# Gapped number row, convolution bias added once, and gather transfers written out one by one

## The reference, cut to what matters

```python
x = x + _L0_gnn_ref(h, ...)   # per edge a two-layer softplus MLP on h[dst] and edge_attr_64, summed by dst
x = x + _L1_gnn_ref(h, ...)   # message = A[type] @ h[src], summed by dst, then a GRU cell on the node
x = x + _L2_gnn_ref(h, ...)   # interaction of p1[src], p1[dst] with 8 basis values, tanh, summed by dst
x = x + _L3_gnn_ref(h, ...)   # two SAGE convolutions

def _sage_conv(x, edge_index, W_l, b, W_r):
    agg = segment_sum(x[src], dst); cnt = segment_sum(ones, dst)
    return (agg / clip(cnt, 1)) @ W_l + b + x @ W_r
h = relu(_sage_conv(x, edge_index, W1_l, b1, W1_r))
return _sage_conv(h, edge_index, W2_l, b2, W2_r)
```

## Time and profile before

| | us |
|---|---|
| median of 3 runs | 7642.43 |
| range of these runs | 7638.81 to 7652.46 |
| the profiled execution | 7640.1 |
| its span, first to last instruction | 7638.6 |
| busy: PE | 6650.0 (87%) |
| busy: POOL | 5038.0 (66%) |
| busy: DVE | 4913.9 (64%) |
| busy: ACT | 3097.5 (41%) |

### The profile page before, as it was taken

One profiled execution on the slowest core, in us unless ns is written; L12 is line 12 of the kernel. 1 busy time (PEld: TensorE's weight loads), 2 busy tenths in 40 slices (PEclk: granted clock), 3 DMA queues, 4 the chain that ended last, 5 costly groups with the idle time before them and its releaser, 6 DMA issues.

```text
span 7638.6 us, 166704 instructions
## 1 busy us (share of the span) xinstructions
PE 6650.0 (87%) x35133; PEld 3361.7 (44%) x35133; DVE 4913.9 (64%) x16097; ACT 3097.5 (41%) x5005; POOL 5038.0 (66%) x6109
## 2 busy tenths in 40 slices
PE   6999999956777777777769999999999899998998
PEld 4666666533333333333323444444444344443443
DVE  7777777646777777777746777777777733332332
ACT  4777777634445555455523333333333201110000
POOL 4544545257777777777747777777777376654776
PEclk9999999975665655665679999999999999998999
DMA  4333333332222222222222222222222266665765
GB/s 125 107 106 107 106 106 107 114 108 85 83 83 84 86 82 87 83 82 85 85 48 59 62 61 61 62 60 61 60 60 62 69 177 172 167 168 157 200 195 156
DMA packets 773997, 769.60 MB, mean 101 GB/s; under 512 B 242490, under 2 KB 585591, under 8 KB 773815
## 3 DMA queue, kind: packets, MB, share of 16 engines
q1 hardware_dynamic: 575703, 589.32, 24.8%
q0 software_dynamic: 147776, 160.99, 10.6%
q10 hardware_dynamic: 50400, 17.87, 1.0%
HBM read 581.15 MB, written 187.29 MB: 101 GB/s over the span
## 4 chain that ended last, share of the span: by engine, by line
PE 58%; POOL 12%; issue 12%; DVE 9%; DMA 4%; DVEq 2%; ACT 2%; ACTq 0%; POOLq 0%; SPq 0%
POOL zone L1045 9%; PE ps L2394 7%; PE ps L2555 7%; PE ps L2184 7%; PE ps L2202 6%; PE ps L2209 5%; PE ps L2386 4%; PE ps L2560 4%; DMA zone<-tab_msg,idx 3%; POOL zone L1085 3%; PE ps L2358 2%; DVE zone L1378 2%; PE ps L2200 2%; PE ps L2413 2%; PE ps L2404 1%
## 5 line engine op out<-in xcount | busy, mean ns | idle before, releaser
L1045 POOL DMA_INDIRECT zone<-tab_msg,idx x1664 | 1721.4, 1034 | 526.9 <-issue 462.3
L1045 POOL DMA_INDIRECT zone<-tab_u,idx x1664 | 1580.7, 950 | 600.1 <-issue 479.9
L2024 ACT ACTIVATE zone<-ps 128x792 fp8e4<-128x792 f32 x1200 | 963.3, 829 | 981.6 <-PE ps L2358 967.8
L1378 DVE TENSOR_TENSOR zone<-ps,zone 128x512 f32<-128x512 f32 x1664 | 1064.0, 686 | 367.0 <-PE ps L2386 335.6
L2184 PE MATMUL ps<-zone 128*128 128x64 f32 (+1 forms) x6656 | 839.2, 284 | 330.1 <-DMA zone<-tab_msg,idx 325.6
L2358 PE MATMUL ps<-zone 128*128 128x396 bf16 x2400 | 905.5, 488 | 234.2 <-ACT zone L2024 146.1
L2184 PEld LDWEIGHTS ps<-zone 128*128 128x128 f32 (+1 forms) x6656 | 758.2, 198 | 490.4 <-issue 438.2
L2394 PE MATMUL ps<-zone,w_bas 128*64 128x512 f32 x3328 | 899.1, 619 | 0.0
L2555 PE MATMUL ps<-zone 128*128 128x512 fp8e4 x3332 | 844.3, 383 | 24.4 <-DMA zone<-adj 14.0
L1663 DVE TENSOR_SCALAR zone<-tT,zone 128x392 bf16<-128x392 f16 x2400 | 779.3, 325 | 0.0
L1337 DVE SCALAR_TENSOR_TENSOR zone<-zone,ps 128x512 f32<-128x512 f32 x832 | 567.0, 687 | 269.8 <-ACT zone L1925 166.9
(11 more groups left out here) (323 smaller groups left out, 8824.5 us busy)
## 6 DMA issues: line engine op xcount, KB each, us to landing
zone<-adj SPq DMA_DIRECT2D x238, 768.0 KB
adj<-zone SPq DMA_DIRECT2D x150, 784.0 KB
zone<-in_dst_row SPq DMA_DIRECT2D x832, 128.0 KB, 2.7
zone<-in_ea_T SPq DMA_DIRECT2D x416, 128.0 KB, 2.6
zone<-src_lin SPq DMA_DIRECT2D x2448, 0.5 KB
zone<-adj SPq DMA_DIRECT2D x34, 896.0 KB
tab_msg<-zone SPq DMA_DIRECT2D x104, 256.0 KB, 2.1
zone<-tab_msg,idx POOLq DMA_INDIRECT x1664
```

The source lines that it names most:

```text
L1045: nc.gpsimd.indirect_dma_start(out=gat(e, u)[:, k, :], out_offset=None, in_=table, in_offset=bass.IndirectOffsetOnAxis(ap=idx[:, u, k:k + ...
L1378: nc.vector.tensor_tensor(zed[:, b % SL, :], bank(2 + b % 2), inter[:, u % 2, b % 2, :], ALU.mult) \
L2024: nc.scalar.activation(staging[m][:, :, at_ * 2 * WN:(at_ + 1) * 2 * WN].rearrange("p b (w d) -> p w b d", w=2), pair_[:, :, 0:CX].rearran ...
```

## The change

1. **Gapped number row.** A second copy of the numbers, `iota_rows`, holds 0 to 391 as 7 rows of 56 at a pitch of 58. `hot_hi` reads this one. Its output is still one run of 392, and `hot_lo` reads the first 128 numbers as before.
2. **Gather written out.** `idx`, `idx_stage`, `idx_pair` and the semaphore `idx_ready` are gone from the two edge stages. POOL's transfers of a stage are written out, 416 x 4, each with a fixed column of `row_i` or `src_i`. POOL still waits for a free buffer (`agg_done`, `inter_done`), and once for `laid_out`.
3. **Bias once.** The one-row matmul and `b_c2` are gone. ACT loads the bias into `b_out` on 128 partitions, and DVE adds it to 98 blocks of `x` in one instruction ahead of `mask_far`.

```diff
+        iota_h = spare[:, 0:P128 // 2].bitcast(FP16)
+        iota_rows = spare[:, P128 // 2:P128 // 2 + ROWS * (WIDE + 2) // 2].bitcast(FP16).rearrange("p (r c) -> p r c", r=ROWS)
...
-            def gather(e, table):
+            def gather(e, table, numbers):
                 with pool.Fori(0, P) as p:
-                    g = pool.snap((P * GATHER[e] + p) * CH)
                     ga = pool.snap((P * e + p) * CH)
                     gi = pool.snap(p * PAIRS)
-
-                    def stage(it, u, _):
-                        pool.wait_ge(idx_ready, done(g, it, u))
+                    for c in range(CH):
+                        it, u = c // RING, c % RING
                         if e != 2:
                             pool.wait_ge(agg_done, done(ga, it, u, RING))
...
-                                in_offset=bass.IndirectOffsetOnAxis(ap=idx[:, u, k:k + 1], axis=0),
+                                in_offset=bass.IndirectOffsetOnAxis(ap=numbers[:, c * TL + k:c * TL + k + 1], axis=0),
                             ).then_inc(gathered[u], 16)
-
-                    chunk_loop(pool, [(0, stage)])
...
             wait_stores(pool, None)
-            gather(1, tab_msg)
+            pool.wait_ge(laid_out, 3)
+            gather(1, tab_msg, row_i)
             wait_flow_end(pool, pool_turn, gru_of, P)
-            gather(2, tab_u)
+            gather(2, tab_u, src_i)
...
-                def idx_pair(it, u, _):
-                    dve.wait_ge(inter_done, done2(g, it, u, RP))
-                    nc.vector.tensor_scalar(idx[:, 2 * u:2 * u + 2, :].rearrange("p s k -> p (s k)"),
-                                            src_i[:, bass.ds((it * RP + u) * (2 * TL), 2 * TL)], 0.0, None, ALU.add) \
-                        .then_inc(idx_ready, 2)
...
-                            nc.vector.tensor_scalar(hot_hi[w % HOTS][:, 0:CW], iota_h[:, 0:CW], codes[:, GW + w:GW + w + 1], None, ALU.is_equal) \
+                            nc.vector.tensor_scalar(hot_hi[w % HOTS][:, 0:CW], iota_rows[:, :, 0:WIDE], codes[:, GW + w:GW + w + 1], None, ALU.is_equal) \
...
             rest_of_sums(0, RC)
+            dve.wait_ge(x_ahead, 32)
+            order(nc.vector.tensor_tensor(x[:, 0:NBS, :], x[:, 0:NBS, :], b_out.unsqueeze(1).to_broadcast([P128, NBS, D]), ALU.add))
             mask_far()
...
+            act.dma_start(b_out, t["c2_b"].to_broadcast([P128, D])).then_inc(x_ahead, 16)
...
-                    mm(bank(1)[:, cols], tT[:, 0, cols], w_c2[:, :], start=True, stop=False)
-                    last = mm(bank(1)[:, cols], ones[0:1, :], b_c2[:, :], start=False, stop=True)
+                    last = mm(bank(1)[:, cols], tT[:, 0, cols], w_c2[:, :], start=True, stop=True)
```

More of the change, by code:

```diff
@@ L224, in build_gnn @@
         w_c2 = sb("w_c2", [H, 2 * D])
-        b_c2 = sb("b_c2", [1, 2 * D])
         bpart = sb("bpart", [3, H], BF16)
@@ L269, in build_gnn @@
         spare = tT[:, 1, :]
-        iota_h = spare[:, 0:IW // 2].bitcast(FP16)
-        S0 = IW // 2
+        ROWS = 7
+        WIDE = CW // ROWS
+        assert CW % ROWS == 0 and WIDE % 2 == 0 and IW == CW
+        iota_h = spare[:, 0:P128 // 2].bitcast(FP16)
+        iota_rows = spare[:, P128 // 2:P128 // 2 + ROWS * (WIDE + 2) // 2].bitcast(FP16).rearrange("p (r c) -> p r c", r=ROWS)
+        S0 = P128 // 2 + ROWS * (WIDE + 2) // 2
+        SPARE_2 = tT[:, 0, SN:GN]
         slot_f = spare[0:GW, S0:S0 + P128]
@@ L277, in build_gnn @@
         e0_list = spare[0:1, S0 + P128 + 32:S0 + P128 + 32 + GW].bitcast(I32)
-        most_rows = spare[:, S0 + P128 + 96:S0 + P128 + 96 + SUB]
-        assert S0 + P128 + 96 + SUB <= GN
+        most_rows = SPARE_2[:, 0:SUB]
+        assert S0 + P128 + 96 <= GN
         lo_f, code_f = (hT[0:GW, 0, SN + n * P128:SN + (n + 1) * P128] for n in range(2))
@@ L309, in build_gnn @@
         assert free_at[0] + AHEAD * TL * W <= at_zone and 1728 + SB * D <= 1920
+        bias_at = NB * D - D
+        assert rel_at + NGC * TL // 2 <= bias_at
+        b_out = zone[:, bias_at:bias_at + D]
         def xp(b, first, last):
@@ L418, in build_gnn @@
         far_in, own_in = gathered, pair_loaded
-        idx_ready = sem("idx_ready")
         selT_built = sem("selT_built")
@@ L672, in build_gnn @@
             (w_c1r[D:D + 1, :], t["c1_b"]),
-            (b_c2[:, D:2 * D], t["c2_b"]),
             (r_pp2T, t["pp_W2_T"]), (r_w1aT, t["pi_W1_T"][:, 0:D]), (r_w1bT, t["pi_W1_T"][:, D:2 * D]),
@@ L682, in build_gnn @@
         ALL_LOADED = 16 * (len(LOADS) + 1)
-        N_CONSTS = 27
+        N_CONSTS = 26
         N_LATE = 3
@@ L945, in _ @@
                                  (w_ih[:, 3 * D:4 * D], 0.0), (w_hh[0:D, 2 * D:3 * D], 0.0),
-                                 (w_uv[D:D + 1, 0:D], 0.0), (b_c2[:, 0:D], 0.0)):
+                                 (w_uv[D:D + 1, 0:D], 0.0)):
                 const(nc.gpsimd.memset(tile_, value))
@@ L1099, in _ @@
         def _(dve):
-            for s_, n in ((idx_ready, RING), (selT_built, RING), (sel_built, RING),
+            for s_, n in ((selT_built, RING), (sel_built, RING),
                           (agg_added, RING), (hid1_ready, RING),
@@ L1318, in selT_stage @@
                 return stage
[L1320 to L1328, removed]
             def edge_mlp(p):
@@ L1388, in add_pair, with plain @@
                             .then_inc(agg_added, 1)
-                return [(0, idx_pair), (4, z_stage(0)), (4, z_stage(1)), (2, selT_pair), (5, sel_pair), (7, add_pair), (4, z_stage(2)),
+                return [(4, z_stage(0)), (4, z_stage(1)), (2, selT_pair), (5, sel_pair), (7, add_pair), (4, z_stage(2)),
                         (4, z_stage(3)), (4, z_stage(4)), (4, z_stage(5)), (4, z_stage(6)), (4, z_stage(7))]
-            def plain(e, numbers):
-                return lambda p: [(0, idx_stage(e, p, numbers)), (1, sel_stage(e, p)),
+            def plain(e):
+                return lambda p: [(1, sel_stage(e, p)),
                                   (ADD_LAG[e], add_stage(e, p, D, (2, 3)))]
@@ L1460, in _ @@
             dve.wait_ge(consts, N_CONSTS + N_LATE)
-            nc.vector.tensor_copy(iota_h, wide_f)
+            nc.vector.tensor_copy(iota_h, wide_f[:, 0:P128])
+            nc.vector.tensor_copy(iota_rows[:, :, 0:WIDE], wide_f.rearrange("p (r c) -> p r c", r=ROWS))
             nc.vector.tensor_copy(slot_f, wide_f[0:GW, 0:P128])
@@ L1806, in mask_far @@
                     match_far(0, 1, u)
-            edge_phase(1, plain(1, row_i), gru_pieces, adjacency)
+            edge_phase(1, plain(1), gru_pieces, adjacency)
             dve.wait_ge(rows_seen, P * (WG * PIECES) + PIECES)
```

## The result

The changed kernel takes **7465.40 us** (median of 4 runs, 7461.1 to 7473.69) beside 7643.43 us for the kernel before, a ratio of 0.9767 (95% interval 0.975 to 0.9784). Its profiled execution took 7463.71 us, with a span of 7462.2. The forecast was 7485.

What follows compares the result with a forecast made beforehand. POOL bounds the GRU stage, PE and DVE the interaction stage, PE the first convolution pass. Terms -4.6 - 90 - 8.2 - 20 - 41 + 6.7 = -157 us give a median of 7485 us; range 7430 to 7578.

Steps and rivals of the forecast that it cites:

- The bound: GRU stage: POOL is the bound, since 1664 gathers take 1034 ns each with 0.30 us of issue before nearly each.
- Part 1, -90: GRU stage: the gapped row slows hot_hi to 412 ns and wins 90 of 140 us lost by gathers; 50 stay.
- Room on DVE: GRU stage: DVE keeps 150 us idle, 2.9 us a turn, which suffices for the slower hot_hi.
- Rival A: GRU stage: DVE takes over or half the loss stays, gaining 45 us instead of 90; 7530 us, chance 0.20.
- Start, -4.6: GRU stage's start: POOL waits for the table's stores alone, so the first gather comes 4.6 us earlier.
- Gap, -8.2: Interaction stage's start: POOL begins at 3890.0 instead of 3898.2, 8.2 us earlier, at least 3.
- Copies in the interaction stage, -20: Interaction stage: the copy leaves the chain at each turn's start, 0.42 us x 47 turns, 20 us; ends 0 and -55.
- Bias matmul, -41: First convolution pass, bound by PE: dropping 196 one-row matmuls saves 41 us, between 36 and 50.
- Bias addition, +6.7: Ahead of mask_far: adding the bias to 6272 elements on DVE makes PE meet its first matching matrix 6.7 us later.
- B: GRU stage: the gapped row does nothing for POOL, only the other parts count, -67 us; 7575 us, chance 0.12.
- D: GRU stage: hot_hi falls to one element a cycle, 616 ns, and DVE bounds the stage; 7823 us, chance 0.04.
- C: All 140 us of the GRU stage go and interaction reaches POOL's pace; 7400 us, half-way 7443, chance 0.07.

Runs made afterwards that it cites:

- e7: Changed kernel with the matching matrices of the GRU and interaction stages made from one SBUF source instead of two, output wrong; 7433.59 us, 0.9724 of before.
- e9: Changed kernel with the 7 rows of 56 read by hot_hi held in fp32 instead of fp16; 7762.91 us, 1.0144 of before.
- e5: Changed kernel with DVE's copies of row numbers and POOL's loop brought back in both gather stages; 7543.92 us, 0.9864 of before.
- e10: Changed kernel with copies of row numbers and POOL's loop back, plus 60 small clears on DVE ahead of the GRU stage; 7491.76 us, 0.9793 of before.

## Why the prediction was right, point by point

- **The bound.** Right: POOL sets the pace of the GRU stage, and a shorter gather shortened it. In the earlier trace rows 299 gathers passed in 400 us; now 310 do, 41.3 us a turn, where 41 was forecast.
- **Part 1, -90.** The stage fell by 83.7 us from the kernel before, and by 95.2 from e1, which undoes part 1 alone. `hot_hi` went to 403 ns (412). The 50 us left over are (984 - 950) x 1664 = 57 by the forecast's own measure, 67 over the shortest gather. The size was right, but **my reason for it was wrong**, so that is luck: I gave it to L1661 by its share of a pair, and L1661 lengthens hardly any gather (0 of 81 before, 7 of 266 now). The lengthened gathers of the changed kernel end behind L1309 and the L1297 that follows it, L1510, L1556, L1631 and others, nearly all with two sources in SBUF, and e7 takes 36 us of the 67 away with `hot_lo` untouched. I had not asked which instructions other than the pair keep POOL waiting; in the earlier trace rows the pair hid them. That its gather ends 0.1 us behind an L1663 says nothing either: going by the addition's 0.82 us, an estimate, it was let in at 2868.5, in the middle of the pairs.
- **Room on DVE.** Its idle time is 2146 - 1730 = 416 us, less L1467's 167 and the 67 in front of L1309, where the idle time that stood at L1326 now lies, some 180 us, 3.5 us a turn in place of 2.9. Rival A didn't come, and by the estimate from e9 it was 93 ns of `hot_hi` away.
- **Start, -4.6.** Measured -5.5, but not shown to be the copies' doing: e5 has them and starts 1.1 us later than the changed kernel. This hit is luck as far as the runs tell.
- **Gap, -8.2.** Measured -11.3, and e5 and e10 give it back (+11.4 and +13.4).
- **Copies in the interaction stage, -20.** Measured -5.7 in POOL's stage and -18.6 in the gap, since PE is now less far behind POOL: -24.3. The two sizes that I hadn't: POOL took over at 40.6 us a turn, not at 40.0. Without the copies DVE's instructions fall in with the gathers, and these lose 32 us in place of 10: by the same count 18.9 behind L1356 and 11.0 behind L1348, where it was 5.0 and 3.4.
- **Bias matmul, -41.** **This is the term that was mis-sized**: 55.5 us. The chain's share of L2480 leaves out what it does to the matmul beside it. Of the 20 us between forecast and result 14 are here.
- **Bias addition, +6.7.** Right, as PE's wait of 7.40 us shows. I had not seen that it holds a gather for 5.7 us as well; there POOL has room.
- **Rivals.** B fell with e1, D's mechanism held with e9 and its price was 69 us too high. C's -140 wasn't reached: even e7, with L1309 and L1356 out of POOL's way, gains only some 33 us more and meets PE and DVE.
- **Slips in the working.** 1.04 ns an element doesn't follow from the earlier trace rows with a fixed part of 208 ns, which gives 1.01 and an L1663 of 604 ns in D (measured 606); the two additions of 1664 and 6272 elements together give 1.04 with 157 fixed. The copy on the chain in the earlier trace rows is 0.48 us, where the sum takes 0.42. And 43 us over 196 matmuls are 0.22 each, not 0.21. None of them changes the forecast by more than 3 us.

## What to carry to other kernels

When an engine that only issues transfers sets the pace, list all the instructions of its neighbour that run while its transfers are long, by their form and the number of sources they read in SBUF, not just the ones that stand in the longest example. The price of a matmul between others is read from the time between its neighbours with it and without it, not from its own share of the chain. And compare kernels stage by stage: a difference in a stage that the edit doesn't touch (e5's 33 us) is a finding of its own, and has to be taken out before a part gets its price.

## What the runs showed of the hardware

- A DVE instruction with two sources in SBUF keeps an indirect gather waiting to its end: an addition of 6.69 us made a gather of 0.94 take 6.67.
- The gather in turn holds up L1348 and the plain `hot_lo` when they begin halfway through it (566 to 698 ns in place of 478, up to 495 in place of 242), but not an instruction with two sources (L1309, 59 times, never over 426).
- The gapped `hot_hi`, at 0.50 ns an element, is as fast per element as L1348 and still lengthens only 1% of the gathers that meet it.
- A source of 7 rows of 56 changes a comparison's form, 310 to 403 ns, and 5 rows of 26 take 265 where 128 in one run took 242; 4 rows of 98 don't change it, 309 ns. From fp32 the 7 rows take 606 ns.
- A loop of DVE's stood still for 3 us twice in 5 of its rounds, with more instruction code being fetched, only by where it lies: 33 us in one pass.
- The same instructions in the GRU stage, behind 60 clears, made it 20 us shorter (e5 and e10), by the gathers that they met.
